# Tile 0 of an adapted layer: the next tile's x1 transposes moved from the second-half to the first-half products

## What is computed

```
H     = x1 @ W.T                                   # x1: [64, 64, 512]
delta = (x1 @ A[adapter].T) @ Bm[adapter].T * scaling[adapter]
z     = H + delta
router_logits = z @ gate_w.T                       # 8 experts
top_w, sel = top_k(router_logits, 2); top_w = softmax(top_w)
out   = x1 + sum over the two experts e of top_w * (silu(z @ g_e) * (z @ u_e)) @ down_e
```

## Time and profile before

| | us |
|---|---|
| median of 3 runs | 1231.99 |
| lowest, highest | 1231.96, 1232.45 |
| the profiled execution's own time | 1234.28 |
| its span in the trace | 1232.5 |
| mean granted TensorE clock, share of full speed | 0.949 |

### The profile page before, as it was taken

The page is one execution under the profiler, slowest core; times in us unless marked ns, Lnnn a source line. Parts: engine busy times, 40 slices in busy tenths (PEclk is TensorE's granted clock), DMA queues, the critical chain, the costliest instruction groups (busy, mean ns, idle before and its releaser), DMA issues. The chain is left out here.

```text
span 1232.5 us, 34938 instructions
## 1 busy us (share of the span) xinstructions
PE 1114.6 (90%) x12488; PEld 1034.1 (84%) x12489; DVE 609.3 (49%) x1161; ACT 504.7 (41%) x994; POOL 740.8 (60%) x1083
## 2 busy tenths in 40 slices
PE   2699999999999998799999459999999999999995
PEld 2689989999989997688998449989898989899994
DVE  9746777767777664335444403333333333333332
ACT  3346777667776665344443112222222222222221
POOL 6668999998999986022433424545455555555553
PEclk9659999999999999689999869999999999999998
DMA  6134554544555543734534513575656565644443
GB/s 260 50 104 154 182 202 159 197 169 152 203 182 174 182 134 142 288 112 142 167 126 144 184 43 69 107 191 144 148 146 148 138 154 130 167 84 71 82 78 58
DMA packets 65921, 177.70 MB, mean 144 GB/s; under 512 B 12656, under 2 KB 21752, under 8 KB 62304
## 3 DMA queue, kind: packets, MB, share of 16 engines
q1 hardware_dynamic: 40736, 127.65, 29.7%
q0 software_dynamic: 19200, 38.94, 17.3%
q10 hardware_dynamic: 5952, 10.65, 2.3%
HBM read 105.84 MB, written 71.38 MB: 144 GB/s over the span
## 5 line engine op out<-in xcount | busy, mean ns | idle before, releaser
L1685 POOL TENSOR_TENSOR idle<-small 128x1 f32<-128x1 f32 x284 | 94.3, 332 | 206.5 <-DMA out<-result,scatter_at 104.3
L958 POOL TENSOR_TENSOR in_lo<-inner,in_hi 128x512 fp32r<-128x512 f32 x128 | 175.5, 1373 | 42.2 <-ACT in_hi L1106 41.9
L1763 PE MATMUL banks<-slots,zt_hi 128*128 x568 | 191.1, 336 | 4.7 <-DVE zt_lo L1852 3.0
L1765 PE MATMUL banks<-slots,zt_lo 128*128 x568 | 184.4, 325 | 0.0
L1764 PE MATMUL banks<-slots,zt_hi 128*128 x568 | 183.6, 323 | 0.0
L1194 DVE TENSOR_TENSOR inner<-silu,banks 128x512 f32<-128x512 f32 x128 | 87.7, 685 | 128.7 <-ACT silu L1101 126.1
L1864 DVE TENSOR_TENSOR hid<-silu_g,banks 128x352 f32<-128x352 f32 x71 | 37.0, 521 | 209.7 <-PE banks L1765 209.7
L1708 POOL DMA_INDIRECT out<-result,scatter_at x71 | 113.6, 1600 | 24.0 <-issue 18.9
L1763 PEld LDWEIGHTS banks<-slots,zt_hi 128*128 128x128 f32 x568 | 107.7, 190 | 7.2 <-issue 6.8
L1830 ACT ACTIVATE zt_hi<-banks 128x512 fp32r<-128x512 f32 x72 | 43.0, 598 | 168.9 <-PE banks L1752 168.9
L1764 PEld LDWEIGHTS banks<-slots,zt_hi 128*128 128x128 f32 x568 | 108.2, 191 | 0.0
(11 more groups left out here) (239 smaller groups left out, 3388.9 us busy)
## 6 DMA issues: line engine op xcount, KB each, us to landing
late_dram<-split_part SPq DMA_DIRECT2D x32, 816.0 KB, 4.3
slots<-late_dram SPq DMA_DIRECT2D x24, 1088.0 KB
raw_part<-in_late_w SPq DMA_DIRECT2D x16, 816.0 KB
x_t<-in_x_t SPq DMA_DIRECT2D x16, 512.0 KB, 3.4
x_both<-in_x_tok SPq DMA_DIRECT2D x16, 512.0 KB, 5.8
x_both<-in_x_res SPq DMA_DIRECT2D x16, 512.0 KB, 3.3
x1t_dram<-x_both SPq DMA_DIRECT2D x16, 512.0 KB, 5.7
x<-x1t_dram SPq DMA_DIRECT2D x16, 512.0 KB
```

The lines of the kernel that those rows point to most:

```text
L958: nc.gpsimd.tensor_tensor(in_lo[:, cs, :], inner[u % 2][:, :, :], in_hi[:, cs, :].bitcast(F32), ALU.subtract).then_inc(in_done, 1)
L1685: nc.gpsimd.tensor_tensor(idle[:, at:at + 1], small[:, 0:1], small[:, 0:1], ALU.add)
L1763: nc.tensor.matmul(psum[bank][:, 0:FD], zt_hi[:, k, :], w_high, start=(k == 0), stop=False)
L1765: ins = nc.tensor.matmul(psum[bank][:, 0:FD], zt_lo[:, k, :], w_high, start=False, stop=(k == DK - 1))
```

## The change

In tile 0, and there alone, the four transposes of tile 1's x1 no longer stand ahead of the second-half products but ahead of the four first-half products, one each. On ScalarE the four `high` of tile 1 stand together behind the copy of (3,1), and each `token_rows` stands ahead of a first-half copy. VectorE's, GpSimd's and SyncE's programs are as before. No instruction is added or left out.

```diff
--- before.py
+++ after.py
@@ -1396,8 +1396,9 @@
+                    behind = isinstance(t, int) and t == 0
                     for s in range(2):
-                        if has_next:
+                        if has_next and not behind:
                             transpose(t + 1, s)
                         product(s, 1, range(DK))
@@ -1405,10 +1406,12 @@
                     for s in range(2):
                         product(s, 1, [DK])
                     for s in range(2, LSUB):
-                        if has_next:
+                        if has_next and not behind:
                             transpose(t + 1, s)
                         product(s, 1, range(DK + 1))
                     for s in range(LSUB):
+                        if behind:
+                            transpose(t + 1, s)
                         product(s, 0, range(DK + 1))
                         if s == LSUB - 2:
                             ranks(t)
@@ -1464,11 +1468,16 @@
                     for s in range(2, LSUB):
-                        if has_next:
+                        if has_next and not behind:
                             high(t + 1, 1 - b, s)
                             token_rows(t + 1, s)
                         copy(s, 1)
+                    if behind:
+                        for s in range(LSUB):
+                            high(t + 1, 1 - b, s)
                     for s in range(LSUB):
+                        if behind:
+                            token_rows(t + 1, s)
                         copy(s, 0)
                         if s == LSUB - 2:
                             shares(t)
```

## The result

The changed kernel is slower: 1237.35 us in the median of 20 runs against 1232.40 us for the kernel before in 20 runs beside them. The ratio is 1.0036 with a 95% interval of 1.0021 to 1.0052, so 4.4 us with 2.6 to 6.4. The prediction was 5.3 us more, 1237.3.

A forecast was written before the change was run, and what follows sets the result against it. TensorE, busy 90% of the span, was taken as the bound. Later x1 +3.5, low clock +2.4 and covered gap -0.6 gave +5.3 us on 1231.99, so 1237.3 us, range 1232.0 to 1240.2.

The forecast's parts named there:

- Tile 0's gain: Tile 0, mark being its last `a` product's start (520.75): last product ends around 540.1 (541.7 at low clock) instead of 544.73.
- The wait at `ranks`: Tile 0, TensorE: `ranks` waits for VectorE's choice, behind the low parts; a new stall of 2.1 us.
- The issue of the load: Tile 0, SyncE: load of tile 2's x1 issued at 539.1 to 539.6 against 536.91, 2.2 to 2.7 us later.
- The load's travel: Load of tile 2's x1, issue to arrival: 8.73 us plus 2.9 (0 to 2.9) for the z store beside it.
- x1's shift: Tile 1's first transposes: start at 551.0 instead of 547.47, 3.5 us later, bounds -0.4 and +4.7.
- The clock and its cover: Tile 1 behind the x1 wait: low clock costs +2.4 us (1.7 to 3.1), covering TensorE's small gap, -0.6 (0 to -1.2).
- That all moves along unchanged behind tile 1: Behind tile 1: the next load's issue and need shift together, so the +5.3 us reaches the layer's end.
- The gain was not kept: Rival, tile 1: x1 arrives before 542.8, TensorE starts 4.6 us earlier, 1227.4 us; chance 0.05.
- The arrival at par: Rival, tile 1: the z store gives way, x1 arrives at 547.35, sum +1.0, 1233.0 us; chance 0.16.
- Tile 2's wait neither went away nor doubled: Two rivals, tile 2: 2.20 us stall goes, 1233.4 us, chance 0.06; ScalarE's lateness shows once more, 1241.2 us, chance 0.08.
- The fifth: Rival, tile 0: a step ahead of the products waits, so the 4.75 us stays unfilled; 1234.1 us; chance 0.03.

The follow-up runs named there:

- number 2: Changed kernel, but in tile 0 VectorE makes the routing's choice ahead of tile 1's four low parts; ratio 1.0005 against the kernel before.
- 4: Changed kernel, but tile 1's x1 has a place of its own and tile 2's is loaded a tile earlier; ratio 0.9988 against the kernel before.
- 9: Changed kernel with 32 extra matmuls filling TensorE's wait ahead of tile 1's first transpose; ratio 1.0031 against the kernel before.
- number 1: Changed kernel, but ScalarE issues tile 0's z store in tile 1, behind the first copy of x1 rows; ratio 1.0002 against the kernel before.
- number 12: Changed kernel with tile 0's choice ahead of the low parts and its z store issued in tile 1; ratio 0.9996 against the kernel before.
- number 10: Kernel before, but GpSimd issues tile 0's eight table writes some 9 us later; ratio 1.0008 against the kernel before.
- the second pair: Kernel before and changed kernel, both unchanged, profiled once more; ratios 0.9993 and 1.0029 against the kernel before.
- 11: Changed kernel with tile 0's four transposes moved earlier, the last ahead of `ranks`, and a place of its own for tile 1's x1; ratio 0.9956 against the kernel before.
- number 8: Changed kernel with tile 0's transposes earlier, the last ahead of `ranks`, and its z store issued in tile 1; ratio 0.9936 against the kernel before.
- 5: Kernel before, unchanged, profiled once more; ratio 0.9993 against the kernel before.
- 6: Changed kernel, unchanged, profiled once more; ratio 1.0029 against the kernel before.
- 3: Kernel before in its own order, but tile 1's x1 has a place of its own and tile 2's is loaded a tile earlier; ratio 0.9956.

## Why the prediction was right, point by point

The mechanism came as forecast: the wait for x1 moved from tile 0 to tile 1 and grew. That the median, 1237.35 us, meets the 1237.3 is luck beyond that. The ratio's interval spans 2.6 to 6.4 us, and errors in the terms cancelled, as the points below show.

**Tile 0's gain.** Predicted end of tile 0: 19.35 us behind the mark (540.1 - 520.75); measured 19.1. The wait for the copy of (0,1) was put at 0.3 us, and the jump from 519.70 to 520.10 instead of 519.82 is 0.28.

**The wait at `ranks`.** Put at 2.1 us, measured 1.66 and 1.64. The cause is as written, VectorE's order: with the choice first (number 2) it is gone. TensorE was there 0.1 us later than written, and the choice was ready 0.4 us earlier. The clock did not fall behind it in either profile of the changed kernel, but it did in numbers 4 and 9.

**The issue of the load.** Put at 2.2 to 2.7 us later, measured 2.0 and 1.9. That the exponential and its table load hide behind the transpose is right, but only by a margin of 0.85 us (ScalarE's wait before its last copy), and number 2 showed them as the next bound.

**The load's travel.** The sum had 8.73 + 2.9 = 11.6 us, the measured is 12.5. The 8.73 was right (8.7 in number 1, 8.2 in number 12). The z store was mis-sized: 3.8 us, above my upper bound of 2.9, which came from the store's own stretch alone. The traffic ended 3.7 us later with the store beside it (number 1), against the 3.0 us that the store takes alone; why the two together need more is open. The half a us from the traffic's end to the arrival, which stands in the bounds of 8.0 and 9.7, had no row; the profiles show 1.3 us in the changed kernel and 1.1 in number 1 up to TensorE's start.

**x1's shift.** Predicted +3.5 us, measured +3.95 (30.67 - 26.72) and +3.81 (30.52 - 26.71). The wait itself was put at 6 to 8 us and is 8.66 and 8.54, since x1 came 0.3 to 0.4 us later and tile 0 ended 0.3 us earlier than written.

**The clock and its cover.** Predicted +2.4 and -0.6. Number 9 against number 12 gives 2.0 for the clock, and number 10 against the first profile 1.2 for ScalarE's lateness, the end of my bounds. From x1 to tile 2 the changed kernel took 18.9 us against 17.8, +1.1, and +1.4 in the second pair, where I had +1.8. So the sum was right by errors that offset each other, the store taken too small against the issue taken too late and the clock's net price taken too high: +5.3 predicted at tile 2, +5.05 and +5.2 measured. That all moves along unchanged behind tile 1 is shown on the third chip alone (numbers 9, 11 and 12).

**The rivals.** The gain was not kept: TensorE was ready 3.9 us behind the issue (538.0 less 534.14), and the shortest way from issue to use in any profile is 8.1 us (number 8). The arrival at par did not happen because the z store did not give way (number 1). Tile 2's wait neither went away nor doubled through the change (numbers 5 and 6). The fifth did not come either: TensorE went on 0.23 us behind the mark.

**The pages.** The rule that transfers issued from different engines interleave on the same DMA engines (Trainium skill, "DMA: Bandwidth & Descriptors", "Issuing engines are not separate DMA queues") was what decided; the runs agree, with 12.5 us beside the store and 8.7 without. The advice to leave no long idle gaps between matmuls (Trainium skill, "TensorE: Matmul & The Clock Gate", "Why this matters for your kernels") holds as well, but for the sum of all gaps: this change filled one of 4.75 us and opened one of 8.66.

## What to carry to other kernels

A wait in the first tile can be the visible end of a chain that runs through one buffer from tile to tile. Before filling it, ask what the moved steps release (here: the buffer of the next load) and how much reserve that release has; here the load was there some 24.9 us behind the mark (16.2 and the 8.7 of number 1) for a need at 26.7, a reserve of 1.9 us. The change put the issue 2.0 us later, had the store cost 3.8 us, and brought the need 4.9 us forward. If a prefetch cannot be issued earlier, give the first one a place of its own, and place the releasing steps ahead of everything that they do not need, here ahead of `ranks`, of the exponential and of a store that shares the DMA engines.

## What was not expected of the hardware

ScalarE starts its first product copies of a tile late on two of the three chips, and in the first pair too, and not at all on the third. Where TensorE's clock is high the first copy of a tile starts 7.0 to 7.4 us behind the tile's first `a` product on the third chip (tile 2 of numbers 9, 10 and 12). In the kernel before it is 8.0 us in tile 1 and 9.6 in tile 2, and 11.1 in tile 2 of number 5, so it is some 1 to 4 us late. TensorE's wait for it is 0.6 to 3.8 us in most tiles. A layer's tile takes 19.3 us on the third chip and 20.4 to 26 on the others, and from the mark to the layer's last product it is 157.7 us in number 10 and 181.7 in number 5. That is 24 us, about the difference of the whole kernels (1220 against 1242 and 1244 us); part of it is the low clock behind these waits, as in tile 2. The profile names no releaser for it ("remote"), here in tile 2 of the kernel before:

```profile
574.78 0.39 ACT L1450 ACTIVATE staging<-banks 128x260 f32<-128x260 f32 x1 [2.89 <-remote]
576.22 0.39 ACT L1450 ACTIVATE staging<-banks 128x260 f32<-128x260 f32 x1 [1.05 <-remote]
```

Its cause is open. It matters for such comparisons: the changed kernel, with its wait for x1 and the low clock behind it, showed none of it in tile 1, and numbers 3 and 4, which start tile 1's products earlier and at the high clock, showed 2.21 and 3.01 us.
